# Node stage of a graph layer: the sine product in four pieces on GpSimd, links spread, x in one layout, the last groups normalised on three engines

## The chip, the cores and the metric

The kernel runs on one core of a Trainium2 chip. The metric is the device time of one execution in microseconds (us); the median of three runs is 1848.68 (1848.46 to 1850.75). VectorE (DVE), ScalarE (ACT), TensorE (PE), GpSimd (POOL) and SyncE (SP) each run their own program in order and wait for each other on semaphores.

## The reference

50,000 nodes with 160 features, 50,000 edges. An edge stage gathers the source nodes' features, multiplies them with edge weights and adds them to the destination nodes; the kernel keeps that sum, already multiplied with `lin2`, in an accumulator `acc` in device memory. The node stage, which alone is changed, computes for each node

```
angle = 0.1 * (mid_s @ lin3_w) / sqrt(96) * node_attr        # one number a node
y     = x + cos(angle) * attr * (x @ sc) + sin(angle) * attr * conv
out   = (y - mean(y)) / sqrt(var(y) + 1e-5)                  # over the 160 features
```

`conv` (160 columns) and the angle before `attr` (column 161) come out of `acc`.

## The kernel before

Nodes are taken in tiles of 128, one node a partition. Four tiles are a group (512 nodes, `G` = 4), and there are 98 groups. Groups are taken in batches: 2 and 5 groups, twelve long batches of 7, then 5 and 2. Groups in a batch are counted from 0 here. What is small and the same for all tiles (angles, sines, variances) is computed once a batch, on 28 numbers a partition in a long one; what has 160 columns is computed a group or a tile at a time.

SyncE loads, for each batch, the x rows (`xn_sb`, L288), the last 32 columns of x once more in a dense layout (`xl_sb`, L289) and the accumulator (`cs_sb`, a part of `shared`, L297), three batches deep, and behind each batch's loads it issues stores of finished groups (L303), each of which waits for its normalisation. So loads that stand behind a store wait for it too.

TensorE transposes x (L519, L520) and multiplies it with `sc` (L529, L533); ScalarE copies the transposes out of PSUM in between (`copy_transposed`, L597).

VectorE computes the angle, reduced to -pi to pi, in six dependent links a batch (`angle`, L761 to L778); ScalarE takes the sines (L605 to L608); VectorE multiplies them with the node attribute (`scale_trig`, L788: the trig product). The links of batch b+1 are spread between the tiles of batch b.

GpSimd then multiplies `conv` with the sine, a group at a time (`conv_times_sine`, L409: the sine product) and adds x (`add_x`, L415: the x addition); the product of a group is issued ahead of the addition of the group before it. VectorE makes y out of TensorE's PSUM, the cosine and that sum (`y_tile`, L830, four a group) and takes statistics of it one group later (`stats_tile`, L840, four a group).

When a batch's statistics are there, VectorE computes the variance in six links (`variance`, L797 to L812, in the first two groups of the next batch; its fifth link writes `vareps`, L810), GpSimd raises it to the power -1/2 (`power`, L402, behind the x addition of group 4 of the next batch), VectorE makes the shift (`mean_shift`, L819, behind group 5), and ScalarE normalises y, four tiles a group, one group for each group that goes on (`normalize`, L618); what is left at the end it does in one go. `times_sine`, `x_added`, `y_done`, `eps_done`, `rstd_done`, `shift_done` and `norm_done` are the semaphores of these steps.

## Time and profile before

| | us |
|---|---|
| median of 3 runs | 1848.68 |
| profiled execution | 1855.24 |
| its span, first to last instruction | 1853.4 |

Busy shares of the span: TensorE 70%, GpSimd 73%, VectorE 57%, ScalarE 41%. The page has the span in 40 slices of 46 us. The edge stage fills the first 31, up to about 1465 us; there the accumulator's last scatters end, and DMA moves 60 to 70 GB/s. The node stage fills the last 9, at 150 to 315 GB/s:

```profile
DVE  4654544544445555555555555565554198777785
ACT  3433333332333333333333333333332035666668
POOL 3347777767777777777777777777775489888885
DMA  7974444444444444444444444444445557778763
GB/s 287 357 258 62 63 63 60 63 61 59 62 61 65 69 66 69 70 70 69 68 69 69 70 69 68 68 69 69 69 69 156 159 207 270 265 266 315 280 221 150
```

A digit is the busy share of an engine in a slice, in tenths (9 is 90% or more); DMA is the mean over 16 DMA engines. In the last slice ScalarE alone is near full.

### The profile page before, as it was taken

To read this page: it belongs to the slowest core of one execution; us is meant where nothing else is said; L and a number is where in the kernel's file an instruction comes from. 1 tells how busy PE (TensorE), PEld (TensorE's weight loads), DVE (VectorE), ACT (ScalarE), POOL (GpSimd) and SP (SyncE) were. 2 spreads that over 40 slices of the span, in tenths; PEclk is the share of its full clock that TensorE was granted. 3 is DMA by queue.
4 is the path that set the end of the run, shared out by engine and by line. 5 is a ranking of instruction groups with operands and counts; after the bars stand their busy time and mean duration, and the time that the engine had idled before them with its cause. 6 is when DMAs were issued, how large, how long until landed. Compare 5 with 4: busy or idle time off the path is not lost.

```text
span 1853.4 us, 34160 instructions
## 1 busy us (share of the span) xinstructions
PE 1303.1 (70%) x8134; PEld 1136.0 (61%) x8134; DVE 1048.9 (57%) x4746; ACT 751.1 (41%) x1715; POOL 1358.1 (73%) x1004
## 2 busy tenths in 40 slices
PE   7767666666676876777677777768776277777773
PEld 5656666565565766666566666657665156666563
DVE  4654544544445555555555555565554198777785
ACT  3433333332333333333333333333332035666668
POOL 3347777767777777777777777777775489888885
PEclk9988888887778899989998889898998588888887
DMA  7974444444444444444444444444445557778763
GB/s 287 357 258 62 63 63 60 63 61 59 62 61 65 69 66 69 70 70 69 68 69 69 70 69 68 68 69 69 69 69 156 159 207 270 265 266 315 280 221 150
DMA packets 166687, 230.68 MB, mean 124 GB/s; under 512 B 50225, under 2 KB 135281, under 8 KB 163057
## 3 DMA queue, kind: packets, MB, share of 16 engines
q1 hardware_dynamic: 91088, 164.49, 27.1%
q0 software_dynamic: 75264, 64.68, 26.0%
q10 hardware_dynamic: 288, 1.00, 0.1%
q8 instruction: 17, 0.28, 0.1%
q14 instruction: 30, 0.24, 0.0%
HBM read 132.67 MB, written 97.40 MB: 124 GB/s over the span
## 4 chain that ended last, share of the span: by engine, by line
DMA 51%; issue 19%; POOL 12%; DVE 7%; PE 5%; ACT 3%; POOLq 1%; SPq 1%; DVEq 0%; ACTq 0%
DMA acc<-shared,row_sb 30%; DMA shared<-x_odd,src_sb 9%; DMA shared<-acc 7%; POOL shared L344 6%; DMA acc<-zeros 5%; POOL acc L360 5%; ACT shared L618 2%; PE XTZ L499 2%; DVE shared L830 2%; DVE ang L761 1%; DVE stats L840 1%; POOL rstd L402 1%; POOL shared L409 1%; POOL shared L415 1%; DVE turns L767 0%
## 5 line engine op out<-in xcount | busy, mean ns | idle before, releaser
L360 POOL DMA_INDIRECT acc<-shared,row_sb x392 | 644.8, 1645 | 234.0 <-issue 139.7
L499 PE MATMUL XTZ<-constants_sb,shared 128*128 128x128 f32 x588 | 127.1, 333 | 387.6 <-DMA shared<-x_odd,src_sb 387.5
L722 DVE TENSOR_TENSOR shared<-shared 128x192 f32<-128x192 f32 x196 | 70.5, 360 | 543.3 <-ACT shared L578 540.5
L499 PEld LDWEIGHTS XTZ<-constants_sb,shared 128*128 128x128 f32 x588 | 71.6, 161 | 423.5 <-DMA shared<-x_odd,src_sb 420.2
L344 POOL DMA_INDIRECT shared<-xa,src_sb x196 | 202.2, 1032 | 123.6 <-DMA src_sb<-src 56.3
L588 ACT COPY shared<-XTZ 128x384 f32<-128x384 f32 x196 | 93.9, 479 | 458.6 <-PE XTZ L499 458.6
L443 PE MATMUL OC<-shared 128*128 128x161 f32 x1176 | 242.7, 352 | 2.4 <-DVE shared L686 1.2
L344 POOL DMA_INDIRECT shared<-x_odd,src_sb x196 | 196.2, 1001 | 59.7 <-issue 46.0
L453 PE MATMUL OC<-constants_sb,shared 128*128 128x193 f32 x784 | 229.5, 379 | 0.0
L443 PEld LDWEIGHTS OC<-shared 128*128 128x128 f32 x1176 | 207.9, 230 | 10.0 <-issue 6.7
L618 ACT ACTIVATE shared<-shared,shift,rstd 128x160 f32<-128x160 f32 x392 | 170.4, 510 | 51.8 <-DVE shift L819 51.8
L455 PEld LDWEIGHTS OC<-constants_sb,shared 128*128 128x128 f32 x784 | 162.4, 219 | 0.0
L484 PE MATMUL W<-constants_sb,shared 64*128 64x192 f32 x784 | 157.9, 351 | 0.0
L455 PE MATMUL OC<-constants_sb,shared 128*128 128x97 f32 x784 | 155.8, 284 | 0.0
L566 ACT COPY shared<-OC 128x386 f32<-128x386 f32 x196 | 94.4, 482 | 144.9 <-PE OC L455 144.9
L453 PEld LDWEIGHTS OC<-constants_sb,shared 128*128 128x128 f32 x784 | 147.9, 225 | 0.0
L474 PE MATMUL FPT<-constants_sb,shared 128*128 128x160 f32 x784 | 147.0, 312 | 0.6 <-ACT shared L588 0.6
L559 ACT COPY shared<-OC 128x322 f32 (+1 forms) x196 | 83.9, 428 | 146.4 <-PE OC L443 146.4
L529 PE MATMUL OC<-constants_sb,xnt_sb 128*128 128x160 f32 x392 | 77.3, 349 | 82.1 <-ACT xnt_sb L597 58.7
L409 POOL TENSOR_TENSOR shared<-shared,trig_a 128x640 f32<-128x640 f32 x98 | 122.7, 1259 | 13.3 <-DVE trig_a L788 13.3
L415 POOL TENSOR_TENSOR shared<-shared,xn_sb 128x640 f32<-128x640 f32 x98 | 129.2, 1326 | 0.0
L692 DVE CUSTOM_DVE_ANT_0 shared<-shared,constants_sb 128x256 f32<-128x256 f32 (+1 forms) x392 | 124.5, 353 | 0.1
(78 smaller groups left out, 2744.4 us busy)
## 6 DMA issues: line engine op xcount, KB each, us to landing
acc<-zeros SPq DMA_DIRECT2D x50, 644.0 KB, 5.8
out<-shared SPq DMA_DIRECT2D x98, 320.0 KB, 5.1
xn_sb<-xa SPq DMA_DIRECT2D x12, 2254.0 KB, 9.1
shared<-acc SPq DMA_DIRECT2D x12, 2254.0 KB, 16.1
dstrow_sb<-dst_rows SPq DMA_DIRECT2D x196, 128.0 KB, 3.4
acc<-shared,row_sb POOLq DMA_INDIRECT x392
xl_sb<-x_last SPq DMA_DIRECT2D x12, 448.0 KB, 9.8
xn_sb<-xa SPq DMA_DIRECT2D x2, 1610.0 KB, 9.3
```

What stands on the lines that cost most here:

```text
L344: pool.indirect_dma_start(out=x_sb[:, g.slot(UNROLL), j * ROWA:(j + 1) * ROWA], out_offset=None, in_=table, in_offset=bass.IndirectOffsetO ...
L360: pool.indirect_dma_start(out=acc, out_offset=bass.IndirectOffsetOnAxis(ap=row_sb[:, slot, j:j + 1], axis=0), in_=comb_sb[:, slot, j, :], ...
L409: pool.tensor_tensor(out=cs, in0=cs, in1=sine, op=ALU.mult).then_inc(times_sine, 1)
L415: pool.tensor_tensor(out=cs, in0=cs, in1=xn_sb[:, b % LOADED, rows, 1:ROWA], op=ALU.add).then_inc(x_added, 1)
L443: last = nc.tensor.matmul(COMB[:, j * ROWA:(j + 1) * ROWA], same_sb[:, e.slot(), b, :], feat_sb[:, e.slot(UNROLL), f, 0:ROWA], start=start ...
L453: nc.tensor.matmul(OUT[:, o:o + OUTW], pt_sb[:, d.slot(), (2 + j) * P:(3 + j) * P], lin2_b_sb[:, :], start=True, stop=False)
L455: last = nc.tensor.matmul(OUT[:, o + NV:o + OUTW], pt_sb[:, d.slot(), j * P:(j + 1) * P], lin2_a_sb[:, :], start=False, stop=True)
L474: nc.tensor.matmul(F[:, j * ROW:(j + 1) * ROW], xt_sb[:, k.slot(), j * P:(j + 1) * P], lin1_a_sb[:, :], start=j == 0, stop=False)
L484: last = nc.tensor.matmul(W[:, j, 0:NW], h_sb[j * NS:(j + 1) * NS, k.slot(), :], fc_w2_sb[j * NS:(j + 1) * NS, :], start=True, stop=True)
L499: last = nc.tensor.transpose(XT[:, b * P:(b + 1) * P], x_sb[:, a.slot(UNROLL), column:column + P], ident_sb[:, :])
L618: last = nc.scalar.activation(y[:, j, :], y[:, j, :], ACT.Identity, bias=shift[:, b % 2, n:n + 1], scale=rstd[:, b % 2, n:n + 1])
L692: last = nc.vector.tensor_tensor_reduce(out=junk_sb[:, 2 * j:2 + j, :].rearrange("p b e -> p (b e)"), in0=same_sb[:, d.slot(), 2 * j:2 + j ...
```

## The change

Only the node stage and the host's layout of x are edited.

- GpSimd's sine product of a group becomes four `tensor_scalar` of one tile each, which take the sine as a number per partition. The x addition becomes two instructions, of the first 128 columns and of the last 32 of the four tiles.
- `power` becomes `root_of`. It is issued behind the first of the four products that group 3's turn issues (those of group 4), and so ahead of group 3's x addition. In batches of fewer than four groups it stands behind the last group.
- VectorE's links stand behind each y tile, one link of each chain at a time, and variance links behind single statistics. The trig product is two instructions.
- x comes in one array, `x_node`: for each group of a partition, the first 128 columns of its four tiles, then the last 32 of all four, then the four attributes. `x_last` and its loads are gone.
- The last batches have 4, 2 and 1 groups instead of 5 and 2.
- The last 14 groups are normalised by three engines: tile 0 by ScalarE, tiles 1 and 2 by GpSimd, tile 3 by VectorE. Their stores wait for all three. GpSimd does groups 84 to 90 behind the power of the batch of two, then the last power, then groups 91 to 97; VectorE does its tiles behind the last variance.
- `rstd` and `shift` have four buffers instead of two, y has 20 instead of 18.

```diff
+STAGED = 4
+Y_RING = 20
+TAIL_GROUPS = 2 * BATCH
-    small = [2, BATCH - 2]
-    sizes = small + [BATCH] * ((groups - 2 * BATCH) // BATCH) + small[::-1]
+    first, last = [2, BATCH - 2], [BATCH - 3, 2, 1]
+    sizes = first + [BATCH] * ((groups - 2 * BATCH) // BATCH) + last
...
                 sp.wait_ge(norm_done, s + 1)
+                if s >= NG - TAIL_GROUPS:
+                    sp.wait_ge(norm_pool, s + 1 - (NG - TAIL_GROUPS))
+                    sp.wait_ge(norm_dve, s + 1 - (NG - TAIL_GROUPS))
...
+            def conv_times_sine(b, i, j):
+                n = i * G + j
+                tile = pool.tensor_scalar(cs_sb[:, b % LOADED, n, 0:ROW], cs_sb[:, b % LOADED, n, 0:ROW],
+                                          trig_a[:, b % 2, 1, n:n + 1], None, ALU.mult)
+                if j == G - 1:
+                    tile.then_inc(times_sine, 1)
...
             for b in range(NB):
                 g, count = BATCHES[b]
+                behind = root_of(b - 1) if b else iter(())
                 pool.wait_ge(triga_done, b + 1)
-                conv_times_sine(b, 0)
+                for j in range(G):
+                    conv_times_sine(b, 0, j)
                 for i in range(count):
-                    if i + 1 < count:
-                        conv_times_sine(b, i + 1)
-                    add_x(b, i)
-                    if i == min(4, count - 1) and b >= 1:
-                        power(b - 1)
-            power(NB - 1)
+                    links = behind if i > 2 else iter(())
+                    for j in range(G):
+                        if i + 1 < count:
+                            conv_times_sine(b, i + 1, j)
+                        next(links, None)
+                    for half in range(2):
+                        add_x(b, i, half)
+                        next(links, None)
+                for _ in behind:
+                    pass
+            for s in range(NG - TAIL_GROUPS, BATCHES[NB - 3][0]):
+                normalize_tail(s)
+            for _ in root_of(NB - 1):
+                pass
+            for s in range(BATCHES[NB - 3][0], NG):
+                normalize_tail(s)
...
-                    for half in range(2):
-                        y_tile(b, i, 2 * half)
-                        y_tile(b, i, 2 * half + 1)
-                        next(ahead, None)
+                    for j in range(G):
+                        y_tile(b, i, j)
                         if i:
                             next(behind, None)
+                        next(ahead, None)
...
             for _ in variance(NB - 1):
                 pass
+            for s in range(NG - TAIL_GROUPS, BATCHES[-1][0]):
+                normalize_tail(s)
             mean_shift(NB - 1)
+            for s in range(BATCHES[-1][0], NG):
+                normalize_tail(s)
```

GpSimd's program in a long batch before, from the sine product of group 4 on (L409 is a sine product, L415 an x addition, L402 the power, each of a whole group or batch):

```order
L409 TENSOR_TENSOR shared<-shared,trig_a 128x4x160
L415 TENSOR_TENSOR shared<-shared,xn_sb 128x4x160 [waits times_sine]
L409 TENSOR_TENSOR shared<-shared,trig_a 128x4x160
L415 TENSOR_TENSOR shared<-shared,xn_sb 128x4x160 [waits times_sine]
L402 TENSOR_TENSOR rstd<-vareps,minus_half 128x28 [waits norm_done,eps_done]
L409 TENSOR_TENSOR shared<-shared,trig_a 128x4x160
L415 TENSOR_TENSOR shared<-shared,xn_sb 128x4x160 [waits times_sine] x2
L409 TENSOR_TENSOR shared<-shared,trig_a 128x4x160 [waits triga_done]
```

The same stretch now, from the first tile's product of group 4 on (L412 is the product of a tile, L424 a piece of an x addition, L406 the power):

```order
L412 TENSOR_SCALAR shared<-shared,trig_a 128x160
L406 TENSOR_TENSOR rstd<-vareps,minus_half 128x28 [waits norm_done,eps_done]
L412 TENSOR_SCALAR shared<-shared,trig_a 128x160 x3
L424 TENSOR_TENSOR shared<-shared,xn_sb 128x4x128 [waits times_sine]
L424 TENSOR_TENSOR shared<-shared,xn_sb 128x4x32
L412 TENSOR_SCALAR shared<-shared,trig_a 128x160 x4
L424 TENSOR_TENSOR shared<-shared,xn_sb 128x4x128 [waits times_sine]
L424 TENSOR_TENSOR shared<-shared,xn_sb 128x4x32
L412 TENSOR_SCALAR shared<-shared,trig_a 128x160 x4
L424 TENSOR_TENSOR shared<-shared,xn_sb 128x4x128 [waits times_sine]
```

The power has moved from behind group 4's x addition to ahead of group 3's: the additions of groups 3 and 4 and the products of groups 4 and 5 have gone behind it.

GpSimd's program at its end before, from the first product of the batch of two on (the last two powers are those of the batches of five and two):

```order
L409 TENSOR_TENSOR shared<-shared,trig_a 128x4x160 [waits triga_done]
L409 TENSOR_TENSOR shared<-shared,trig_a 128x4x160
L415 TENSOR_TENSOR shared<-shared,xn_sb 128x4x160 [waits times_sine] x2
L402 TENSOR_TENSOR rstd<-vareps,minus_half 128x20 [waits norm_done,eps_done]
L402 TENSOR_TENSOR rstd<-vareps,minus_half 128x8 [waits norm_done,eps_done]
```

Its end now, from the products of the batch of two on (the powers of 16 and 8 elements are those of the batches of four and two, L435 is a tile's normalisation):

```order
L412 TENSOR_SCALAR shared<-shared,trig_a 128x160 x7
L424 TENSOR_TENSOR shared<-shared,xn_sb 128x4x128 [waits times_sine]
L424 TENSOR_TENSOR shared<-shared,xn_sb 128x4x32
L424 TENSOR_TENSOR shared<-shared,xn_sb 128x4x128 [waits times_sine]
L424 TENSOR_TENSOR shared<-shared,xn_sb 128x4x32
L406 TENSOR_TENSOR rstd<-vareps,minus_half 128x16 [waits norm_done,eps_done]
L412 TENSOR_SCALAR shared<-shared,trig_a 128x160 [waits triga_done]
L412 TENSOR_SCALAR shared<-shared,trig_a 128x160 x3
L424 TENSOR_TENSOR shared<-shared,xn_sb 128x4x128 [waits times_sine]
L424 TENSOR_TENSOR shared<-shared,xn_sb 128x4x32
L406 TENSOR_TENSOR rstd<-vareps,minus_half 128x8 [waits norm_done,eps_done]
L435 TENSOR_SCALAR shared<-shared,rstd,shift 128x160 [waits shift_done]
```

A power has come to stand between the last two batches' products, and 28 tiles of normalisation (the first of them is the last row here) follow the power of the batch of two.

VectorE's program in group 1 of a long batch before (L830 is a y tile, L840 statistics, L773 and L778 angle links, the other rows variance links up to `vareps`):

```order
L830 SCALAR_TENSOR_TENSOR shared<-W,trig_a,shared 128x160 x2
L773 SCALAR_TENSOR_TENSOR ang<-turns,ang 128x28
L799 TENSOR_TENSOR m<-stats 128x28
L830 SCALAR_TENSOR_TENSOR shared<-W,trig_a,shared 128x160 x2
L778 TENSOR_SCALAR red<-ang 128x28
L802 SCALAR_TENSOR_TENSOR mdiff<-mdiff 128x28
L840 BN_STATS stats<-shared 128x6 x2
L805 TENSOR_SCALAR m2eps<-m 128x28
L840 BN_STATS stats<-shared 128x6 x2
L810 TENSOR_TENSOR vareps<-mdiff,m2eps 128x28
```

The same group now (L870 is a y tile, L880 statistics, L808 and L813 angle links, L835 to L848 variance links):

```order
L870 SCALAR_TENSOR_TENSOR shared<-W,trig_a,shared 128x160
L835 TENSOR_TENSOR mdiff<-stats 128x28
L808 SCALAR_TENSOR_TENSOR ang<-turns,ang 128x28
L870 SCALAR_TENSOR_TENSOR shared<-W,trig_a,shared 128x160
L837 TENSOR_TENSOR m<-stats 128x28
L813 TENSOR_SCALAR red<-ang 128x28
L870 SCALAR_TENSOR_TENSOR shared<-W,trig_a,shared 128x160
L840 SCALAR_TENSOR_TENSOR mdiff<-mdiff 128x28
L870 SCALAR_TENSOR_TENSOR shared<-W,trig_a,shared 128x160
L843 TENSOR_SCALAR m2eps<-m 128x28
L880 BN_STATS stats<-shared 128x6
L848 TENSOR_TENSOR vareps<-mdiff,m2eps 128x28
```

The variance starts one link later and ends three statistics earlier.

## Rows read from the trace of the kernel before

**Rows 1.** Chain of waits, rounds of the node stage: start us, us, what.

```profile
1658.87 1.14 DVE ang L761
...
1668.28 14.87 DMA shared<-acc
...
1683.17 5.03 DVE ang L761
```

**Rows 2.** Busy time by engine (x instructions), granted clock, DMA share, GB/s, one load.

```profile
1641.50:1658.80 17.30, 15.07 (x100) 12.58 (x98) 10.43 (x40) 13.36 (x31) 17.30 (x13) 0.88 0.97 369
```

**Rows 3.** VectorE timeline, first angle link, first and last of twelve rounds: start, us.

```profile
1503.58 0.81 DVE L761 TENSOR_TENSOR ang<-shared,xn_sb 128x28 f32<-128x28 f32 x1
...
1811.43 0.78 DVE L761 TENSOR_TENSOR ang<-shared,xn_sb 128x8 f32<-128x8 f32 x1
```

**Rows 4.** Waits in these rounds: engine, line, releaser: us in total, times, longest.

```profile
DVE ang L761 <- DMA shared<-acc: 17.9, 8, 3.1
```

**Rows 5.** GpSimd timeline, the power and what follows it in one round.

```profile
1665.90 4.80 POOL L402 TENSOR_TENSOR rstd<-vareps,minus_half 128x28 f32<-128x28 f32 x1 [3.46 <-DVE vareps L810]
1670.67 1.25 POOL L409 TENSOR_TENSOR shared<-shared,trig_a 128x640 f32<-128x640 f32 x1
1671.89 2.61 POOL L415 TENSOR_TENSOR shared<-shared,xn_sb 128x640 f32<-128x640 f32 x2
```

**Rows 6.** VectorE timeline of the same round.

```profile
1665.65 0.17 DVE L810 TENSOR_TENSOR vareps<-mdiff,m2eps 128x28 f32<-128x28 f32 x1
...
1669.10 0.25 DVE L788 TENSOR_TENSOR trig_a<-trig,xn_sb 128x56 f32<-128x56 f32 x1
...
1673.30 1.26 DVE L830 SCALAR_TENSOR_TENSOR shared<-W,trig_a,shared 128x160 f32<-128x160 f32 x4 [0.96 <-issue]
1674.48 1.00 DVE L840 BATCH_NORM_STATS2 stats<-shared 128x6 f32<-128x160 f32 x4
1675.39 0.36 DVE L819 SCALAR_TENSOR_TENSOR shift<-msum,rstd 128x28 f32<-128x28 f32 x1
```

**Rows 7.** VectorE timeline of a round whose loads had landed.

```profile
1546.32 0.35 DVE L819 SCALAR_TENSOR_TENSOR shift<-msum,rstd 128x28 f32<-128x28 f32 x1
...
1551.49 0.68 DVE L830 SCALAR_TENSOR_TENSOR shared<-OC,trig_a,shared 128x160 f32<-128x160 f32 x2 [2.74 <-PE OC L533]
...
1556.55 1.30 DVE L797 TENSOR_TENSOR mdiff<-stats 128x28 f32<-128x28 f32 x1
...
1560.92 0.17 DVE L810 TENSOR_TENSOR vareps<-mdiff,m2eps 128x28 f32<-128x28 f32 x1
```

**Rows 8.** GpSimd groups by form: count, busy us, mean ns, idle before.

```profile
L415 POOL TENSOR_TENSOR shared<-shared,xn_sb 128x640 f32<-128x640 f32 x98 | 129.2, 1326 | 0.0
...
L409 POOL TENSOR_TENSOR shared<-shared,trig_a 128x640 f32<-128x640 f32 x98 | 122.7, 1259 | 13.3 <-DVE trig_a L788 13.3
...
L402 POOL TENSOR_TENSOR rstd<-vareps,minus_half 128x28 f32<-128x28 f32 x12 | 57.7, 4807 | 41.8 <-DVE vareps L810 41.8
...
L328 POOL MEMSET zeros<- 128x1288 f32 x1 | 1.2, 1172 | 0.3 <-POOLq L977 0.3
...
L329 POOL MEMSET half_pi<- 128x1 f32 x1 | 0.1, 103 | 0.0
```

**Rows 9.** DMA issues on the page: count, KB each, us to landing.

```profile
out<-shared SPq DMA_DIRECT2D x98, 320.0 KB, 5.1
...
xl_sb<-x_last SPq DMA_DIRECT2D x12, 448.0 KB, 9.8
```

**Rows 10.** VectorE's last-but-one long `vareps`, and ScalarE's last stretch, from their timelines.

```profile
1795.96 0.16 DVE L810 TENSOR_TENSOR vareps<-mdiff,m2eps 128x28 f32<-128x28 f32 x1
...
1827.31 23.13 ACT L618 ACTIVATE shared<-shared,shift,rstd 128x160 f32<-128x160 f32 x56 [1.31 <-DVE shift L819]
```

**Rows 11.** Waits in the whole node stage, columns as in rows 4.

```profile
DVE shared L830 <- POOL shared L415: 7.0, 2, 3.9
```

More of the change, by code:

```diff
@@ L393, in _, with root_of @@
                 scatter(n, n % RING)
-            def power(b):
-                g, count = BATCHES[b]
+            def root_of(b):
+                n = BATCHES[b][1] * G
                 pool.wait_ge(eps_done, b + 1)
-                if b >= 2:
-                    over, groups = BATCHES[b - 2]
+                if b >= STAGED:
+                    over, groups = BATCHES[b - STAGED]
                     pool.wait_ge(norm_done, over + groups)
-                pool.tensor_tensor(out=rstd[:, b % 2, 0:count * G], in0=vareps[:, b % 2, 0:count * G],
-                                   in1=minus_half[:, 0:count * G], op=ALU.pow).then_inc(rstd_done, 1)
@@ new lines, in root_of, with add_x @@
+                yield
+            def conv_times_sine(b, i, j):
[4 more added lines that the diff above has]
+                    tile.then_inc(times_sine, 1)
+            def add_x(b, i, half):
+                rows = slice(i * G, (i + 1) * G)
+                if half == 0:
+                    pool.wait_ge(times_sine, BATCHES[b][0] + i + 1)
+                    cs, x = cs_sb[:, b % LOADED, rows, 0:P], xn_sb[:, b % LOADED, i, 0:A_END]
+                else:
+                    cs, x = cs_sb[:, b % LOADED, rows, P:ROW], xn_sb[:, b % LOADED, i, A_END:X_END]
+                part = pool.tensor_tensor(out=cs, in0=cs, in1=x.rearrange("p (j c) -> p j c", j=G), op=ALU.add)
+                if half:
+                    part.then_inc(x_added, 1)
@@ new lines, in normalize_tail @@
+            def normalize_tail(s):
+                b = max(k for k in range(NB) if BATCHES[k][0] <= s)
+                i = s - BATCHES[b][0]
+                pool.wait_ge(shift_done, b + 1)
+                y = y_sb[:, s % Y_RING, :, :]
+                for j in (1, 2):
+                    n = i * G + j
+                    last = pool.tensor_scalar(y[:, j, :], y[:, j, :], rstd[:, b % STAGED, n:n + 1], shift[:, b % STAGED, n:n + 1],
+                                              ALU.mult, ALU.add)
+                last.then_inc(norm_pool, 1)
@@ L842, in stats_tile, with normalize_tail @@
                     tile.then_inc(stats_done, 1)
+            def normalize_tail(s):
+                b = max(k for k in range(NB) if BATCHES[k][0] <= s)
+                i, j = s - BATCHES[b][0], G - 1
+                dve.wait_ge(shift_done, b + 1)
+                y, n = y_sb[:, s % Y_RING, :, :], i * G + j
+                nc.vector.tensor_scalar(y[:, j, :], y[:, j, :], rstd[:, b % STAGED, n:n + 1], shift[:, b % STAGED, n:n + 1],
+                                        ALU.mult, ALU.add).then_inc(norm_dve, 1)
             for _ in angle(0):
@@ L865, in _ @@
                             scaled = True
-                    for half in range(2):
+                    for j in range(G):
                         if before:
-                            stats_tile(*before, 2 * half)
-                            stats_tile(*before, 2 * half + 1)
-                        next(ahead, None)
-                        next(behind, None) if i or half else None
+                            stats_tile(*before, j)
+                            if i:
+                                next(behind, None)
                     if i == min(5, count - 1) and not shifted:
@@ L891, in layouts @@
     xa[:n, 0], xa[:n, 1:1 + NV], xa[:n, 1 + NV:] = node_vec1[:, 0], x[:, NS:], x[:, :NS]
+    x_node = np.empty((rows, ROWA), f32)
+    for g, count in batches_of(tiles // G):
+        part = xa[g * G * P:(g + count) * G * P].reshape(P, count, G, ROWA)
+        blocks = (part[..., 1:1 + P], part[..., 1 + P:], part[..., 0])
+        x_node[g * G * P:(g + count) * G * P] = np.concatenate(
+            [block.reshape(P, count, -1) for block in blocks], axis=2).reshape(-1, ROWA)
     src_p = np.zeros(rows, np.int32)
```

63 lines of the change are left out of this document (30 added, 33 removed).

## The prediction

> **What bounds the kernel now.** I read the page first, for where the node stage lies, then the chain of waits in it, then each engine's timeline over two of its rounds, the groups by form, the waits, and the instruction order. The profiled execution took 1855.24 us, 6.6 more than the median of 1848.68; its span is 1853.4. I work out differences from its rows and add them to the median.
>
> The stage runs from about 1465 to the end. A round is a batch of seven groups. The chain shows the same loop in most rounds: the accumulator lands, VectorE starts the angle chain, and 24.3 us later the next accumulator lands; its transfer holds 14.9 us of that [rows 1]. The sixteen DMA engines are 0.97 busy then, at 369 GB/s [rows 2]. So DMA ends last there, because SyncE issues that load only behind a store that waits for ScalarE's normalisation, and that ScalarE program stands behind the sines of the angle chain. From the first angle link of the first long batch to that of the batch behind the last long one 12 rounds pass, 1811.43 - 1503.58 = 307.85, or 25.65 each [rows 3]. In that whole stretch VectorE waited for this DMA 17.9 us [rows 4].
>
> A second loop lies close behind. From the end of `vareps` (1665.82) GpSimd starts the power 0.08 later and its next instruction 4.77 after that [rows 5], so the result is there at 4.85. Then come one sine product and one x addition; y of group 5 follows at 1673.30, 7.5 after `vareps`, having waited 0.96 for that addition [rows 6]. Four y tiles take 1.18 and four statistics 0.91 from start to start, so shift starts at 9.6. ScalarE's normalisation waits for shift, its PSUM copy behind it holds TensorE up, and the first y of the next batch starts 1546.32 to 1551.49 = 5.17 after shift. From there to the end of `vareps` 1551.49 to 1561.09 = 9.6 pass [rows 7]. Sum 24.3: this is the time of a round when its data are there.
>
> **The change, part by part.** Time 0 is again the end of `vareps`.
>
> *The power's place.* The order shows it: before, the power stood behind the x addition of group 4; now it stands behind the first of four products of group 4, ahead of the x additions of groups 3 and 4. Everything behind a GpSimd wait waits with it. VectorE is in group 1 when it finishes `vareps`, so groups 3 to 5 now all wait for the power, where only group 5 did.
>
> *The products.* No `tensor_scalar` on GpSimd stands in the trace. A memset of 1288 elements takes 1172 ns and of one 103, so 0.83 ns an element and 0.1 fixed: 160 elements make 0.23. The product's and the addition's 640 elements take 1259 and 1326, so 1.8 to 1.9 ns an element: 160 make 0.39 to 0.41 [rows 8]. It reads one tensor, where a memset reads none and the addition two; I take 0.30, between them, and keep 0.23 and 0.41. The x addition in two pieces costs one more fixed 0.1: 1.28 (1671.89 to its end, two in 2.61) becomes 1.38, of which the long piece is 1.08.
>
> The Trainium skill (GPSIMD Engine Reference, Engine selection) says that an op with one input runs on GpSimd at about line rate, and one with two at about half of VectorE's speed. No row here shows a GpSimd op with one input. By that rule the product would be near the low end and the sum that of the first rival below.
>
> *A round now.* 4.85 + three products 0.9 + addition 1.38 = 7.1: y of group 3 starts at 7.2. VectorE is ready for it at 2.9 (a link 0.1, three statistics 0.7, four y 1.2, four statistics 0.9), so it now stands 4.3 us where it didn't. Four y: 8.4. Then the two trig products. Before, this step cost 0.25, since it fell under the power, which leaves VectorE alone (1669.10 lies inside it). Now GpSimd is running its additions, and a VectorE instruction with two SBUF operands waits for the end of GpSimd's running one: `mdiff` of 28 elements took 1.30 us in such a place [rows 7]. I take 1.5 for both: 9.9. Statistics: 10.8. Groups 4 and 5 then go at VectorE's 2.09 (their additions arrive at 9.7 and 12.3): shift at 15.0, next batch's y at 20.2. From there to `vareps`: eight y 2.4, now five statistics instead of eight 1.1, eleven links at about 0.1 (a row's start to the next row's start) 1.2, and waits for the port. The pieces of GpSimd's work are shorter (0.30 against 1.26), so I take 0.3 for each of the four links that fall into them: 5.9 instead of 9.6. A round: 26.1. GpSimd itself needs 7 x 2.58 + 4.85 = 22.9, less than that.
>
> *The loads.* 448 KB of each round's loads go [rows 9]: 0.46 MB at 380 GB/s (369 over 0.97) make 1.2 us off the DMA loop. With fewer port waits in the angle chain that loop falls from 24.3 to below 22, so the second loop covers it and the saving counts nothing; if the second loop were gone, DMA would give 2 us a round. The x rows are as many bytes as before; TensorE's transposes and the additions read as many elements; four buffers for rstd and shift and twenty for y lift waits that no row shows. Nothing for all these.
>
> *Rounds:* 12 x (26.1 - 25.65) = +5.4. *The first short batches:* their power is short (8 and 20 elements), and links there fall between GpSimd's pieces as the one of 1.30 does; four of them at 0.6 less each make -2.5, an estimate.
>
> *The end.* `vareps` of the last but one long batch ended at 1796.12, the span 57.3 later. ScalarE normalised 56 tiles in one stretch, 1827.31 to 1850.44, and nothing but the last store ended later [rows 10]. Now, from the same point: 26.1 `vareps` of the last long batch; power 30.9; addition of group 94's x (behind the power) 32.3; y and trig 33.8; eight products and an addition 37.6; y, angle links, statistics 40.7; y and links to `vareps` of the batch of four 43.1; power of 16 elements (4.77/28 each) 2.8: 45.9. Only behind this power come the products of the last group: 48.5. y, statistics, links 51.1; power of 8 elements 52.5. Only now GpSimd starts to normalise group 84, though its shift has been there since 35. VectorE starts its own share behind shift, four statistics (0.9) and six links that wait for GpSimd's 0.35 pieces (2.1): 55.9 with its first tile. SyncE's stores wait for three engines in order, so all fourteen start after that: 14 x 327,680 B = 4.6 MB at 380 GB/s are 12.1, and 2.1 from the last byte to the end (3.0 before, with 0.9 of transfer): 70.1. GpSimd's 28 tiles of 0.35 (a product and a second operand and operation, an estimate) and a power of 0.7 from 52.5 on, and the 3.0 of a store, would allow 66.0. So ScalarE's 23 us become a chain of small batches through three engines: +12.8.
>
> Sum: 5.4 - 2.5 + 12.8 = +15.7, so **1864**.
>
> **Rivals.**
> 1. *The product costs 0.23.* Additions arrive earlier and the port waits shrink: y of group 3 at 7.0, shift at 14.2, next y at 19.3, `vareps` at 24.9: 12 x -0.75 = -9; the start -3, the end +12. Sum 0: 1849. For it: the memset's rate. Against: nothing is read there.
> 2. *The product costs 0.39 to 0.41.* Additions then set the pace (2.98 each): shift at 15.5, the next y at 20.7, round 27.0: +16; start -1.5, end +14: 1877. For it: the rate of the product now.
> 3. *VectorE loses the port to back-to-back GpSimd work.* The angle link took 1.14 in one round and 5.03 in another [rows 1]; the latter ended only when GpSimd paused. With short pieces the first link could wait from 20.5 until GpSimd's pause at 22.9 in half the rounds: 12 x 1.2 = 14 more: 1878. It decides when the link's mean stays above 1.5 us.
> 4. *The power's new place costs nothing,* since shorter port waits bring `vareps` early enough: rounds of 24.3 as when data are there: -16, start -2.5, end +12.8 or, if the stores don't pile up, +9: 1839 to 1843, faster. For it: VectorE waited for GpSimd's addition only 7.0 us in the stage before [rows 11]. Against: the order, in which three groups stand behind the power.
>
> **How the numbers follow.** Forecast (1856 to 1872) 0.45, rival 1 (1843 to 1853) 0.20, rival 2 0.15, rival 3 0.10, rival 4 0.10. What a measurement can tell is about 0.2%, 3.7 us. Rival 1 gives 0.13 to "same", 0.04 to faster and 0.03 to slower. Faster 0.14, same 0.13, slower 0.73. Range: 1843 takes in most of rival 1, 1884 rivals 2 and 3.
>
> **What the profile after would show.** VectorE's y waits for GpSimd's x addition 3 to 4.5 us in each long batch, some 45 us in all, from 7.0. The wait of the angle link for the accumulator falls below 4 us. The angle links of long batches stand 26 us apart. A GpSimd `tensor_scalar` takes 0.3. The last fourteen stores are issued in the last 16 us, and ScalarE is done before them. I am wrong if rounds take under 25, or if the stretch from the last but one long `vareps` to the end is under 62.

## The result, and the profile after

The changed kernel took 1977.43 us (median of 3 runs, 1976.55 to 1982.93) against 1848.68: a ratio of 1.0704, interval 1.0678 to 1.073. It is slower by 129 us, where 16 were forecast and 1884 was the end of the range. The profiled execution took 1982.93 us, its span is 1981.1; against the profiled execution of before that is 127.7 more.

The page has GpSimd busy for 78% of the span. The chain that ended last, followed back over the whole span, goes through GpSimd for a third, where before it did for 12%:

```profile
DMA 41%; POOL 33%; issue 19%; PE 4%; DVE 2%; POOLq 1%; ACT 0%; SPq 0%; DVEq 0%; ACTq 0%
```

VectorE's first angle links (L794) of the stretch that [rows 3] bounds, from its timeline:

```profile
1511.56 0.19 DVE L794 TENSOR_TENSOR ang<-shared,xn_sb 128x28 f32<-128x28 f32 x1
...
1920.92 0.16 DVE L794 TENSOR_TENSOR ang<-shared,xn_sb 128x8 f32<-128x8 f32 x1
```

Twelve rounds take 1920.92 - 1511.56 = 409.36 us, 34.1 each instead of 25.65. So 101.5 of the 127.7 us are in the rounds. From 1920.92 to the end of the span it is 60.2 us where before had 42.0 from 1811.43: +18.2. The start up to 1511.56, counted from the first link at 1467.88, is 43.7 instead of 34.0: +9.7. The edge stage ended 1.7 earlier. Together 127.7.

The same stretch in the table of busy time (engines, granted clock, DMA share, GB/s), which answers [rows 2]:

```profile
1512.00:1921.00 409.00, 257.70 (x1421) 212.44 (x1421) 224.63 (x853) 189.43 (x431) 409.00 (x516) 0.77 0.48 180
```

GpSimd is busy in 409 of 409 us. DMA, which was 0.97 busy in one load of before and 0.68 over its twelve rounds, is at 0.48 over these. TensorE, 258 us busy, has a granted clock of 0.77 (before 0.85), a mean between its two levels of 1.2 and 2.4 GHz; that explains little here, since the chain of these rounds has about 1% of its work. One round of the chain, in order of time:

```profile
1689.37 0.66 POOL shared L412
1690.03 4.79 POOL rstd L406
1694.82 2.00 POOL shared L412 x3
1696.83 1.54 POOL shared L424 x2
1698.36 2.67 POOL shared L412 x4
...
1724.32 4.82 POOL rstd L406
```

Where [rows 1] had the accumulator, VectorE and the next accumulator, here stand only GpSimd's instructions, one behind the other: seven times four products (2.67) and two pieces of an addition (1.54), and a power (4.8), make 34.3 by the starts of the rows. The groups by form, which answer [rows 8], have the reason (count, busy us, mean ns):

```profile
L412 POOL TENSOR_SCALAR shared<-shared,trig_a 128x160 f32<-128x160 f32 x392 | 263.2, 689 | 13.0 <-DVE trig_a L824 13.0
L424 POOL TENSOR_TENSOR shared<-shared,xn_sb 128x512 f32<-128x512 f32 x98 | 115.4, 1177 | 0.1
L406 POOL TENSOR_TENSOR rstd<-vareps,minus_half 128x28 f32<-128x28 f32 x12 | 58.0, 4831 | 0.1
L424 POOL TENSOR_TENSOR shared<-shared,xn_sb 128x128 f32<-128x128 f32 x98 | 42.3, 432 | 0.0
L435 POOL TENSOR_SCALAR shared<-shared,rstd,shift 128x160 f32<-128x160 f32 x28 | 13.5, 499 | 0.0
```

A product of 160 elements takes 689 ns. Four of them take over twice the 1259 ns of the one operation that they replace. The normalisation in L435, a `tensor_scalar` of the same shape with a second operand and a second operation, takes 499: less for more work. The waits of the stage are now those behind GpSimd, and answer [rows 4, 11]:

```profile
DVE shared L870 <- issue: 116.2, 40, 6.1
DVE shared L870 <- POOL shared L424: 103.9, 27, 7.1
```

VectorE's y (L870) waited 103.9 us for the additions, 7.0 before. Another 116.2 go to "issue" (5.8 before), for which the profile names no releaser; in the chain above nothing but GpSimd is late. The end, from GpSimd's timeline:

```profile
1949.55 3.04 POOL L406 TENSOR_TENSOR rstd<-vareps,minus_half 128x16 f32<-128x16 f32 x1 [4.22 <-DVE vareps L848]
...
1960.07 1.67 POOL L406 TENSOR_TENSOR rstd<-vareps,minus_half 128x8 f32<-128x8 f32 x1 [3.15 <-DVE vareps L848]
1961.74 7.06 POOL L435 TENSOR_SCALAR shared<-shared,rstd,shift 128x160 f32<-128x160 f32 x14
...
1969.77 6.45 POOL L435 TENSOR_SCALAR shared<-shared,rstd,shift 128x160 f32<-128x160 f32 x14
```

GpSimd works to 1976.2 and the last store follows. This is the chain through GpSimd, VectorE and GpSimd that the prediction drew, with ScalarE's 23 us of [rows 10] gone.

### The profile page after: what moved, and what is told of

Read it like the earlier page. It is cut to its first block, busy times and chain, and to the rows that moved or that the text cites. A ratio compares the mean times of both kernels' runs of the same rounds, so it can differ in the third digit from the quotient of the medians.

```text
span 1981.1 us, 34610 instructions
## 1 busy us (share of the span) xinstructions
PE 1346.7 (68%) x8134; PEld 1171.1 (59%) x8134; DVE 1033.7 (52%) x4791; ACT 736.9 (37%) x1676; POOL 1535.8 (78%) x1425
## 4 chain that ended last, share of the span: by engine, by line
DMA 41%; POOL 33%; issue 19%; PE 4%; DVE 2%; POOLq 1%; ACT 0%; SPq 0%; DVEq 0%; ACTq 0%
DMA acc<-shared,row_sb 29%; POOL shared L412 13%; DMA shared<-x_odd,src_sb 7%; POOL shared L424 7%; POOL shared L348 6%; DMA acc<-zeros 4%; POOL acc L364 4%; POOL rstd L406 3%; PE XTZ L533 2%; POOL shared L435 1%; DVE shared L870 0%; POOLq L71 0%; PE FPT L508 0%; PE OC L487 0%; DMA src_sb<-src 0%
## 5 line engine op out<-in xcount | busy, mean ns | idle before, releaser
L412 POOL TENSOR_SCALAR shared<-shared,trig_a 128x160 f32<-128x160 f32 x392 | 263.2, 689 | 13.0 <-DVE trig_a L824 13.0
L487 PE MATMUL OC<-constants_sb,shared 128*128 128x193 f32 x784 | 234.3, 386 | 0.0
L651 ACT ACTIVATE shared<-shared,shift,rstd 128x160 f32<-128x160 f32 x350 | 153.4, 511 | 190.8 <-DVE shift L857 190.8
L562 PE MATMUL OC<-constants_sb,xnt_sb 128*128 128x160 f32 x392 | 88.0, 383 | 125.9 <-ACT xnt_sb L630 68.0
L489 PEld LDWEIGHTS OC<-constants_sb,shared 128*128 128x128 f32 x784 | 166.7, 224 | 0.0
L562 PEld LDWEIGHTS OC<-constants_sb,xnt_sb 128*128 128x128 f32 x392 | 77.3, 255 | 133.6 <-ACT xnt_sb L630 76.4
L424 POOL TENSOR_TENSOR shared<-shared,xn_sb 128x512 f32<-128x512 f32 x196 | 153.1, 805 | 0.1
L487 PEld LDWEIGHTS OC<-constants_sb,shared 128*128 128x128 f32 x784 | 151.2, 229 | 0.0
L562 PE MATMUL W<-constants_sb,xnt_sb 128*128 128x160 f32 x392 | 86.5, 378 | 88.6 <-DVE shared L870 56.1
```

The source lines that it names most:

```text
L412: tile = pool.tensor_scalar(cs_sb[:, b % LOADED, n, 0:ROW], cs_sb[:, b % LOADED, n, 0:ROW], trig_a[:, b % 2, 1, n:n + 1], None, ALU.mult)
L424: part = pool.tensor_tensor(out=cs, in0=cs, in1=x.rearrange("p (j c) -> p j c", j=G), op=ALU.add)
L487: nc.tensor.matmul(OUT[:, o:o + OUTW], pt_sb[:, d.slot(), (2 + j) * P:(3 + j) * P], lin2_b_sb[:, :], start=True, stop=False)
L489: last = nc.tensor.matmul(OUT[:, o + NV:o + OUTW], pt_sb[:, d.slot(), j * P:(j + 1) * P], lin2_a_sb[:, :], start=False, stop=True)
L562: nc.tensor.matmul(banks[:, h, j * ROW:(j + 1) * ROW], xnt[:, (2 * h + j) * P:(2 * h + j + 1) * P], sc_a_sb[:, :], start=j == 0, stop=False)
L651: last = nc.scalar.activation(y[:, j, :], y[:, j, :], ACT.Identity, bias=shift[:, b % STAGED, n:n + 1], scale=rstd[:, b % STAGED, n:n + 1])
```

## The experiments

| kernel | median us | ratio to before, interval | a round, us |
|---|---|---|---|
| before | 1848.7 | | 25.65 |
| after | 1977.4 | 1.0704 [1.0678, 1.0730] | 34.1 |
| product_whole | 1874.6 | 1.0142 [1.0103, 1.0181] | 26.6 |
| product_two_op | 1893.5 | 1.0219 [1.0182, 1.0256] | 27.6 |
| before_four_products | 1945.0 | 1.0507 [1.0466, 1.0548] | 32.3 |
| power_back | 1870.0 | 1.0125 [1.0086, 1.0163] | 26.55 |
| end_back | 1867.3 | 1.0087 [1.0057, 1.0118] | 27.3 |
| power_end_back | 1865.2 | 1.0087 [1.0053, 1.0120] | 26.75 |
| before_two_adds | 1868.5 | 1.0107 [1.0089, 1.0124] | 26.95 |
| before_links | 1848.3 | 1.0002 [0.9990, 1.0014] | 25.5 |
| pause | 1847.8 | 1.0002 [0.9988, 1.0016] | 25.5 |
| before_pause | 1853.2 | 1.0030 [1.0021, 1.0040] | 25.6 |

A round is a twelfth of the way between the same two angle links as in [rows 3], in the profiled execution. Ratios are to runs of before on the same chip, whose medians were 1849.4 for the kernels of the product, 1852.1 for the three with "back" and 1847.0 for the last four. One of *power_back*'s six runs took 1887.2, the others 1867 to 1873, and its ratio holds that one too.

**The product's form.** *product_whole* is the changed kernel with the one product operation of before:

```
-                n = i * G + j
-                tile = pool.tensor_scalar(cs_sb[:, b % LOADED, n, 0:ROW], cs_sb[:, b % LOADED, n, 0:ROW],
-                                          trig_a[:, b % 2, 1, n:n + 1], None, ALU.mult)
...
+                sine = trig_a[:, b % 2, 1, rows].rearrange("p (g o) -> p g o", o=1).to_broadcast([P, G, ROW])
+                pool.tensor_tensor(out=cs, in0=cs, in1=sine, op=ALU.mult).then_inc(times_sine, 1)
```

> The changed kernel with one edit undone: the sine product of a group is again one tensor_tensor of 640 elements. All else stays, the power's new place and the end on three engines too. Theory (the product of a tile takes 0.67 us, and GpSimd's own program then sets the round): the products fall from 2.67 to 1.22 us a group, GpSimd's program to 7 x (1.22 + 1.55) + 4.83 = 24.2 a round, less than the loop through power, shift and y, which I had at about 26; so 1855 to 1868. Rival (the power's place, the additions in two pieces and the end carry most of the 129 us): the time stays above 1930.

*product_two_op* leaves four products and gives each a second operation that adds nothing:

```
-    trig_a[:, b % 2, 1, n:n + 1], None, ALU.mult)
+    trig_a[:, b % 2, 1, n:n + 1], 0.0, ALU.mult, ALU.add)
```

> The changed kernel, with a second operation in each of the four products: times the sine, plus 0.0 (the same numbers come out). In the changed kernel the product with one operation takes 689 ns and the normalisation with two operations 499 ns on tiles of the same size. Theory A (the form with one operation is the slow one): the product falls to about 0.50, a round to 7 x (2.0 + 1.55) + 4.83 = 29.7, the time to 1915 to 1925. Theory B (something else of the product is slow, its rows of 161 columns or its place): it stays at 0.67 to 0.69 or rises, and the time at 1977 or above.

*before_four_products* puts the four one-operation products of the change into the kernel before, and nothing else of it:

```
...
-                pool.tensor_tensor(out=cs, in0=cs, in1=sine, op=ALU.mult).then_inc(times_sine, 1)
+                for j in range(G):
+                    n = i * G + j
+                    tile = pool.tensor_scalar(cs_sb[:, b % LOADED, n, 0:ROW], cs_sb[:, b % LOADED, n, 0:ROW],
+                                              trig_a[:, b % 2, 1, n:n + 1], None, ALU.mult)
+                tile.then_inc(times_sine, 1)
```

> The kernel before with one edit of the change alone: the sine product of a group in four tensor_scalar of a tile. Theory (GpSimd's program sets the round): 7 x (4 x 0.667 + 1.28) + 4.8 = 32.4 us a round in place of 25.65, 12 x 6.7 = +81 and 5 to 8 in the first batches: 1930 to 1942. Rival (most of the loss lies in the other edits): below 1890.

*probe_pool* is before with 31 operations on GpSimd behind all its work (its time means nothing), among them

```
+            for r in range(4, 8):
+                pool.tensor_scalar(xn_sb[:, 0, r, 0:ROW], src[:, 0, :], one, None, ALU.mult)
+            for r in range(8, 12):
+                pool.tensor_scalar(xn_sb[:, 0, r, 0:ROW], src[:, 0, :], one, two, ALU.mult, ALU.add)
...
+            for r in range(0, 4):
+                pool.tensor_scalar(xn_sb[:, 1, 4 * r:4 * r + 4, 0:ROW], src, one, None, ALU.mult)
```

> The kernel before, with 31 instructions on GpSimd added behind everything else, into x rows that nobody reads any more; their time alone matters, not the kernel's. Tiles of 160 elements, four each: one operation with a number per partition, two operations with two numbers per partition, one operation with a constant, two with a number and 0.0, a tensor_tensor of 160; a tile of 32 elements; four tiles in one instruction with one and with two operations. Theory A (one operation is slow whatever the place): 0.67 for the first, 0.50 for the second and the fourth; the ratio holds for 640 elements. Theory B (rows, buffers or the sine's place make it): first and second alike, near 0.50. If most of the 0.67 is a fixed cost, the tile of 32 stays above 0.5; if it is by element, it takes about 0.2.

The probe's timeline, start and us of each run of equal instructions:

```profile
1841.55 2.67 POOL L436 TENSOR_SCALAR xn_sb<-xn_sb,trig_a 128x160 f32<-128x160 f32 x4 [9.84 <-ACT shared L641]
1844.22 1.83 POOL L438 TENSOR_SCALAR xn_sb<-xn_sb,trig_a 128x160 f32<-128x160 f32 x4
...
1848.35 1.51 POOL L442 TENSOR_SCALAR xn_sb<-xn_sb,trig_a 128x160 f32<-128x160 f32 x4
1849.85 1.35 POOL L444 TENSOR_SCALAR xn_sb<-xn_sb,trig_a 128x32 f32<-128x32 f32 x4
1851.16 1.73 POOL L446 TENSOR_TENSOR xn_sb<-xn_sb 128x160 f32<-128x160 f32 x4
1852.89 7.45 POOL L448 TENSOR_SCALAR xn_sb<-xn_sb,trig_a 128x640 f32<-128x640 f32 x4
1860.33 2.57 POOL L450 TENSOR_SCALAR xn_sb<-xn_sb,trig_a 128x640 f32<-128x640 f32 x3
```

L436 is the product of the change, with every other engine idle: 2.67 for four, as in the kernel. With a second operation and the constant 0.0 (L442) four take 1.51. At 640 elements the one-operation form takes 7.45/4 = 1.86 us (L448) and the two-operation form 2.57/3 = 0.86 (L450). From 160 to 640 elements that is 1.19 us for 480, 2.5 ns an element. With two operations on two columns (L438, 1.83/4, to L450) it is 0.40, 0.8 ns. So the price is the form's and not the neighbours'. The cut into four pieces has its share too: four pieces of 160 cost 2.67 where one of 640 costs 1.86, and with a `tensor_tensor` 1.73 (L446) where one of 640 costs the 1.26 of [rows 8]. Of the 1.4 us that a group's product grew by, 0.6 to 0.9 go to the form and the rest to the cut.

In *product_two_op* the same products take 398 ns in the kernel, less than the 0.50 expected, and 84 us go where 52 to 62 were expected. With *product_whole*, 103 of the 129 us go; at 1874.6 it stays 6 us over its expected range. *before_four_products* has the loss by itself: expected 32.4 a round and at most 1942, measured 32.3 and 1945.0.

```profile
L408 POOL TENSOR_SCALAR shared<-shared,trig_a 128x160 f32<-128x160 f32 x392 | 262.5, 695 | 11.5 <-DVE trig_a L789 11.5
L402 POOL TENSOR_TENSOR rstd<-vareps,minus_half 128x28 f32<-128x28 f32 x12 | 58.1, 4839 | 0.0
```

These are its groups by form: the power had no idle time before it, so `vareps` was always there first and GpSimd alone sets the pace of the rounds. With nothing of the links, the layout or the end changed, this is the cause shown from both sides.

The Trainium skill (GPSIMD Engine Reference, Engine selection) has it that ops with one input run at about line rate there. The two-operation form agrees, with the 0.8 ns an element that a memset takes in [rows 8]; the one-operation form, with the same single tensor, takes 2.5, and the measurement decides.

**What is left: 26 us.** The trace of *product_whole* is the one in which the prediction's other terms can be read, since the product has before's price. Its links, its last stores and its waits:

```profile
1465.92 0.17 DVE L795 TENSOR_TENSOR ang<-shared,xn_sb 128x8 f32<-128x8 f32 x1 [42.11 <-DMA shared<-acc]
...
1497.79 0.82 DVE L795 TENSOR_TENSOR ang<-shared,xn_sb 128x28 f32<-128x28 f32 x1
...
1816.69 0.48 DVE L795 TENSOR_TENSOR ang<-shared,xn_sb 128x8 f32<-128x8 f32 x1
```

```profile
1854.05 11.32 SPq L307 DMA_DIRECT2D out<-shared  x14
```

```profile
DVE shared L871 <- issue: 41.3, 11, 3.8
...
DVE shared L871 <- POOL shared L425: 22.6, 9, 4.2
```

A round is 26.6, the start 31.9 (2.1 shorter), and from 1816.69 to the end 53.2 (11.2 longer). The edge stage ended 3.7 earlier, so between these two profiled executions only 16.5 us lie; that of before was 6.6 above its median, this one 2.5 below. The other 9 us of the 26 are in neither trace. y waits 22.6 us for additions and 41.3 on "issue". Fourteen stores leave in 11.3 us, from 1854.05. One round from `vareps` (L849) to `vareps`, and the chain from 1600 to 1700 by line:

```profile
1635.31 0.16 DVE L849 TENSOR_TENSOR vareps<-mdiff,m2eps 128x28 f32<-128x28 f32 x1
...
1641.98 1.26 DVE L871 SCALAR_TENSOR_TENSOR shared<-OC,trig_a,shared 128x160 f32<-128x160 f32 x4 [3.59 <-issue]
...
1662.40 0.16 DVE L849 TENSOR_TENSOR vareps<-mdiff,m2eps 128x28 f32<-128x28 f32 x1
```

```profile
by line: POOL shared L425 20.0%; POOL rstd L406 19.6%; POOL shared L416 8.5%; DVE shared L871 6.9%; DVE stats L881 6.8%; DVE ang L795 5.6%; PE W L563 4.7%; issue 4.7%; ACT shared L652 4.1%; PE OC L563 3.2%; DVE ang L806 3.1%; DVE turns L800
```

y of group 3 comes 6.5 after `vareps`, having stood 3.59, and the next batch's y, at 1655.69, 20.2 after it. From one `vareps` of a long batch to the next, seven of the eleven stretches take 25.6 to 26.0, two 27.1 to 27.2, and two 28.4; in the last two the first angle link took 3.65 and 3.90. So the forecast's loop through the power, the additions (L425) and y is there. What its parts are worth, the next three ask. Each is *product_whole* with one part, or both, taken back.

*power_back*: the power behind the x addition of group 4 again.

```
-                    links = behind if i > 2 else iter(())
...
-                        next(links, None)
...
+                    if i == min(4, count - 1):
+                        for _ in behind:
+                            pass
...
```

> The changed kernel with the product as one operation (product_whole: 1874.6, rounds of 26.6) and, besides, the power back behind the x addition of group 4. Theory B (the power's new place is what lengthened the rounds of product_whole, since three groups' x additions then stand behind it): the second loop is back near its 24.3, links spread and 448 KB less to load, so rounds of 23.5 to 24.8 and 12 x 2.2 = 26 us less: 1845 to 1860. Rival (the rounds are long because the additions in two pieces and the spread links cost more; the place is indifferent): rounds stay at 26 to 26.6, time 1868 to 1876. The end stays as in product_whole, 15 us longer than before from the last but one long vareps.

*end_back*: ScalarE alone normalises, and the last batches are of five and two groups:

```
-TAIL_GROUPS = 2 * BATCH
+TAIL_GROUPS = 0
...
-    first, last = [2, BATCH - 2], [BATCH - 3, 2, 1]
+    first, last = [2, BATCH - 2], [BATCH - 2, 2]
...
```

> product_whole with the end as before: last batches of five and two groups, and ScalarE alone normalises them. The power stays in its new place. Theory C (the end costs what was worked out, since small batches chain through GpSimd, VectorE and GpSimd again): from the last but one long vareps to the end 57 to 61 us instead of 72.6, rounds as in product_whole (26.0 to 26.6), time 1859 to 1864. Rival (the end is long because the last rounds themselves are late: the power's place acts there too, the split costs nothing): under 4 us gained, 1870 to 1876.

*power_end_back*: both of these edits.

> product_whole with both the power's place and the end as before. What stays of the change is x in one layout, the addition in two pieces, the angle and variance links spread and the deeper buffers. If theories B and C add up: 1874.6 - 26 - 13 = 1832 to 1848, at or under the kernel before, with rounds of 23.5 to 24.8 where those of before are 25.65; the DMA loop is 1.2 us shorter by the 448 KB that it no longer loads. Rival (some of the other parts costs time by itself, above all the addition in two pieces, 0.27 us more a group): rounds over 25.7 and a time of 1850 to 1860.

Theory B fell: with the power back, rounds are 26.55 where they were 26.6. *power_end_back* came out at 1865.2, above the range of its theory and of its rival. What happens there shows on VectorE, in the first angle link of *power_end_back*, and on GpSimd beside it:

```profile
1600.88 6.37 DVE L789 TENSOR_TENSOR ang<-shared,xn_sb 128x28 f32<-128x28 f32 x1 [1.43 <-DMA shared<-acc]
```

```profile
1605.63 1.58 POOL L425 TENSOR_TENSOR shared<-shared,xn_sb 128x512 f32<-128x512 f32 x2
1611.46 4.95 POOL L406 TENSOR_TENSOR rstd<-vareps,minus_half 128x28 f32<-128x28 f32 x1 [4.26 <-DVE vareps L843]
```

The accumulator is there at 1600.88, and the link, of 28 elements, ends at 1607.25: when GpSimd's last addition ends (1607.21) and GpSimd pauses for `vareps`. It is over 5.7 us in six of twelve long batches (six, not the seven that a later expectation names), and each time ends within 0.06 us of GpSimd's pause. This is the prediction's third rival. With the power ahead of the additions the link is short (0.19 to 0.83 in ten of twelve long batches of *product_whole*), and y of three groups waits instead. Over its rounds the chain of *power_back* goes through the accumulator's load (29%) and this link (11%), no longer mainly through power and additions. Either place costs a round as much: the wait moved.

Theory C is not settled by the totals: *end_back* has a ratio 0.0055 lower and *power_end_back* 0.0038, and the intervals overlap. In their traces the stretch from the same link to the end is 44.4 and 42.7 instead of 53.2, so 9 to 10.5 us of the end are there; the rounds of *end_back* came out 0.7 longer in that execution, which took them back.

**The rest of the change.** After all this 13 us stay. Two suspects, each put into before alone. *before_two_adds*:

```
-                pool.tensor_tensor(out=cs, in0=cs, in1=xn_sb[:, b % LOADED, rows, 1:ROWA], op=ALU.add).then_inc(x_added, 1)
+                x = xn_sb[:, b % LOADED, rows, 1:ROWA]
+                pool.tensor_tensor(out=cs[:, :, 0:P], in0=cs[:, :, 0:P], in1=x[:, :, 0:P], op=ALU.add)
+                pool.tensor_tensor(out=cs[:, :, P:ROW], in0=cs[:, :, P:ROW], in1=x[:, :, P:ROW], op=ALU.add).then_inc(x_added, 1)
```

> The kernel before with the x addition in two pieces, 128 and 32 columns of each tile, the layout of x left as it was. GpSimd's work of a round grows by 7 x 0.27 = 1.9 us. Theory E (what is left of the loss in power_end_back, 13 us, comes from this: GpSimd pauses later, so the first angle link waits longer for it): 1855 to 1872, with rounds of 26.2 to 27 and the link over 2.9 us in more than four rounds. Rival (the spread links do it): within 4 us of the kernel before.

*before_links*: VectorE's loop of the changed kernel, of which the core is

```
-                        y_tile(b, i, 2 * half)
-                        y_tile(b, i, 2 * half + 1)
-                        next(ahead, None)
+                        y_tile(b, i, j)
                         if i:
                             next(behind, None)
+                        next(ahead, None)
```

> The kernel before with the angle and variance links of VectorE spread as in the changed kernel, one after each y tile. Theory E: within 5 us of the kernel before, or some us faster, since the chain's six links no longer stand behind four y tiles and statistics. Rival (the spread links cost the 13 us that power_end_back is slower, since more of them stand beside GpSimd's work and wait for the port one by one): 1858 to 1866, rounds over 26.2.

The addition costs some 20 us by itself, the links nothing. The first links of *before_two_adds* as a group:

```profile
L763 DVE TENSOR_TENSOR ang<-shared,xn_sb 128x28 f32<-128x28 f32 x12 | 43.0, 3581 | 18.9 <-DMA shared<-acc 18.9
```

Their mean is 3.58 us, over 4.6 in eight of twelve batches; in before it was 1.96 with four over 2.9. GpSimd's two pieces, a row of before's layout:

```profile
1661.71 1.09 POOL L416 TENSOR_TENSOR shared<-shared,xn_sb 128x512 f32<-128x512 f32 x1
1662.77 0.41 POOL L417 TENSOR_TENSOR shared<-shared,xn_sb 128x128 f32<-128x128 f32 x1
1663.14 1.25 POOL L409 TENSOR_TENSOR shared<-shared,trig_a 128x640 f32<-128x640 f32 x1
```

They take 1.43 from start to start where one addition took 1.28: 0.15 a group, 1.0 us a round, less than the 1.9 that I expected from the changed layout's 1.54. For it the links wait 1.6 us longer each on the mean, and a round takes 1.3 more.

**The link itself.** *pause* is *power_end_back* with one wait on GpSimd, ahead of the product of group 4:

```
+    if i == 3 and count == BATCH and b + 1 < NB:
+        pool.wait_ge(angled, (b + 1) * 5 + 1)
```

> power_end_back with one wait added: in each long batch GpSimd waits, ahead of the product of group 4, until VectorE has done the first link of the next batch's angle chain. In power_end_back that link took 6 us in seven of twelve rounds and each time ended when GpSimd next paused. Theory D (VectorE's first link, with two operands in SBUF, gets nowhere while GpSimd runs products and additions back to back, and the chain of waits goes through it): the link takes under 1 us in the long batches, a round loses about 3 us, from 26.7 to 23.5 to 25 (GpSimd's own work of 24.4 a round is the next bound), time 1835 to 1850 where power_end_back has 1865. Rival (the link is long because something else holds VectorE, or the wait only moves the loss to GpSimd): rounds of 26 to 28, time 1860 or more.

*before_pause* is before with the same two lines.

> The kernel before with the same one wait of GpSimd on the first angle link. There the link took over 2.9 us in four of twelve rounds. Theory D: these four fall under 1 us and about 8 to 13 us go, 1838 to 1845. Rival (before is bound by the load alone, or the wait costs GpSimd as much): 1848 to 1860.

Theory D holds where the link was long. The first links of *power_end_back*, then of *pause*:

```profile
L789 DVE TENSOR_TENSOR ang<-shared,xn_sb 128x28 f32<-128x28 f32 x12 | 43.5, 3621 | 12.4 <-DMA shared<-acc 12.4
```

```profile
L791 DVE TENSOR_TENSOR ang<-shared,xn_sb 128x28 f32<-128x28 f32 x12 | 10.5, 878 | 10.1 <-DMA shared<-acc 9.9
```

33 us of waiting go, GpSimd waits 1.0 us in all for it, and 1865.2 becomes 1847.8 (1.0087 to 1.0002). The rounds fell by 1.3 to 25.5, not to the 23.5 to 25 expected. In before the wait costs GpSimd 9.2 us and the kernel 0.3%; the second row is of `mdiff` there:

```profile
POOL shared L409 <- DVE ang L763: 9.2, 7, 1.6
```

```profile
L799 DVE TENSOR_TENSOR mdiff<-stats 128x28 f32<-128x28 f32 x12 | 16.4, 1364 | 0.0
```

The link fell from 1.96 to 0.43 there, yet rounds stayed at 25.6. The 18 us came back in the links behind it, which now fall into GpSimd's work: `mdiff` takes 1.36 where it took 0.59, and the three angle links behind the first take 0.83 to 0.89 where they took 0.47 to 0.63, together 20.8 us more. The chain of these rounds still goes through the accumulator's load for 45%. The theory's 8 to 13 us for this kernel were wrong. No version beat before by more than a measurement can tell. The one layout of x without the two pieces wasn't tried, so what its 448 KB a round are worth stays open.

## Why the prediction was wrong

**The step that failed** is *The products*: "I take 0.30, between them, and keep 0.23 and 0.41." The product takes 0.69 (0.67 from start to start), outside both ends. The bounds came from a memset and a `tensor_tensor`, and I took a form with one tensor to lie between none and two. The trace had no row of that form, and the range should not have ended at the nearest two: I chose bounds for the count of operands and the price hangs on the form. The two signs of being wrong that I named, a round under 25 and an end under 62, both looked for a kernel faster than forecast. With 0.67 the prediction's own check of GpSimd ("7 x 2.58 + 4.85 = 22.9, less than that") reads 34.3, more than every other loop, and the rounds alone give 12 x 8.6 = +104.

**A second term was too small:** the addition in two pieces was taken as 1.38, from 1.28, and takes 1.54, so 1.8 us a round instead of 0.7. I set it against y alone, where it hardly counts; *before_two_adds* shows that two pieces of even 1.43 cost some 20 us, because the first link waits for GpSimd's pause.

**The round without the product** was forecast at 26.1; *product_whole* has 26.6 on the mean and 25.6 to 26.0 in seven of eleven. Its steps are there too: y of group 3 stands 3.6 where 4.3 were forecast, and the next batch's y follows `vareps` by 20.2, as forecast. The y waits named for the additions are 22.6 us where 45 were forecast; another 41.3 are on "issue". So mechanism and size of this term were right. What it doesn't say is that the place costs nothing that could be had back: put back, the round stays, and the wait moves to the angle link.

**The third rival** had its mechanism right: the link held until GpSimd pauses. It sits in the kernels with the power behind the addition, with 6 us and not 1.2, in two rounds of *product_whole* with 3.7 and 3.9, and in the changed kernel not at all: the link takes 0.2 there with GpSimd never idle.

**The start** (-2.5 forecast, -2.1 in *product_whole*) came out without the product, though no run shows that its cause is the one given; with the product it is +9.7. **The end:** from the last but one long `vareps` on, +12.8 was forecast and *product_whole* has 72.6 against 57.3, so +15.3; the first of the fourteen stores was forecast 55.9 behind that `vareps` (1797.27), so at 1853.2, and left at 1854.05. What stands behind that store is partly luck:

```profile
1858.48 6.50 POOL L436 TENSOR_SCALAR shared<-shared,rstd,shift 128x160 f32<-128x160 f32 x14
```

I let the rate of the stores set the last 12 us. In fact GpSimd's tiles take 0.46 us each, not 0.35, its last ends at 1864.98, and the last store waits for it. Also, the rounds were counted up to a link that lies behind this `vareps`, so my two terms overlap: from the link on, the end is 11.2 longer, and the other 4.1 of the 15.3 are in the rounds as well. In the changed kernel the last fourteen stores leave over 12.2 us, much as in *product_whole*.

**Links spread, buffers, bytes** were put at nothing. For the links *before_links* shows it; the others were not run alone.

## What to carry to other kernels

Where the trace has no row of the very form that a change adds (engine, instruction, number of operations, operand kinds), the cost has no bound from its neighbours: the range must reach to where that engine becomes the bound, and that threshold is easily worked out (here 0.40 us a product, at which 7 x (4 products + the forecast's 1.38) + 4.85 passes 25.65; with the measured 1.54 it is 0.36). Past it, each 0.1 us of a product costs 12 x 2.8 = 34 us, an estimate from the counts above. On an engine that runs back to back, count pieces as well as elements, each at the price of its own form. A wait that was taken out of one of these loops came back in another place twice: with the power put back, and with the pause in before.

## What the runs showed of the hardware

- On GpSimd a `tensor_scalar` with one operation takes 0.67 us for 160 float32 elements and 1.86 for 640; with a second operation 0.38 to 0.50 and 0.86. An operation that does nothing saved 84 us here. A `tensor_tensor` of 160 takes 0.43, less than the one-operation `tensor_scalar`.
- A VectorE instruction on two SBUF operands can stand for several GpSimd instructions, not one: 6.37 us over eight products and additions of at most 1.3 each, until GpSimd paused. The Trainium skill (SBUF — State Buffer, Summary: rules for kernel authors) says that of a VectorE instruction with two SBUF inputs and a GpSimd one that reads SBUF, the one issued second is blocked until the first finishes. `mdiff`'s 1.30 us in [rows 7] agree with that, and the link of 6.37 doesn't; there the measurement decides.
- What lets an instruction through is not settled here. In the changed kernel GpSimd was busy in all of 409 us, and the link, which starts there among one-operation products, took 0.2 us. But in *before_four_products* another VectorE instruction on two SBUF operands (`m`, L800) took 1.3 us in nine of twelve long batches, over two of the same products. And in the changed kernel `m2eps` (L843), with one SBUF operand, took 1.81 on the mean, beside products and an addition, where it took 0.16 before:

```profile
L800 DVE TENSOR_TENSOR m<-stats 128x28 f32<-128x28 f32 x12 | 14.8, 1229 | 0.0
```

```profile
L843 DVE TENSOR_SCALAR m2eps<-m 128x28 f32<-128x28 f32 x12 | 21.7, 1809 | 0.0
```
